# Mixture-of-experts tail of an attention kernel: the order in which POOL issues row gathers and row scatters

## The reference, cut to what is computed

```python
x = layernorm(x + attention(x))          # 2 batches x 1024 tokens x 128, 8 heads, differential attention
# the expert layer, E = 8 experts, cap = 256 tokens per expert and batch
probs = softmax(x @ gate_w)
top_p, top_idx = top_k(transpose(probs), cap)
xin = take_along_axis(x, top_idx)        # the rows that each expert chose
h = gelu(xin @ w1)                       # 128 -> 512
y = (h @ w2) * top_p                     # 512 -> 128
out = zeros().at[top_idx].add(y)         # rows added back where they came from
x = layernorm(x + out)
```

## Time and profile before

| what | us |
|---|---|
| median of 3 runs | 1060.2 |
| lowest, highest of them | 1058.76, 1063.17 |
| the profiled execution's own time | 1051.25 |
| its span, first to last instruction | 1049.5 |
| expert stage: first gather to the landing of the last scatter | 907.88 to 1028.70 |

### The profile page before, as it was taken

One profiled execution on the slowest core, in us unless ns is written; L12 is line 12 of the kernel. 1 busy time (PEld: TensorE's weight loads), 2 busy tenths in 40 slices (PEclk: granted clock), 3 DMA queues, 4 the chain that ended last, 5 costly groups with the idle time before them and its releaser, 6 DMA issues.

```text
span 1049.5 us, 15335 instructions
## 1 busy us (share of the span) xinstructions
PE 888.1 (85%) x4365; PEld 718.0 (68%) x4366; DVE 764.1 (73%) x1183; ACT 581.7 (55%) x1090; POOL 795.6 (76%) x874
## 2 busy tenths in 40 slices
PE   6789999999999999999999999999999732386700
PEld 5577778787877788778877887878788631165500
DVE  6777788877887878788778877888788547574303
ACT  3556667666766576656765666766676331143100
POOL 2567878887888798888888888888799753377762
PEclk9999999999999999999999999999999955599755
DMA  2000000000000000000000000000000152012223
GB/s 71 1 11 11 1 1 22 1 1 0 20 0 0 10 10 0 0 10 10 0 0 10 10 0 0 10 0 0 1 1 1 47 137 65 19 51 36 27 26 87
DMA packets 31856, 18.57 MB, mean 18 GB/s; under 512 B 4512, under 2 KB 30272, under 8 KB 31824
## 3 DMA queue, kind: packets, MB, share of 16 engines
q1 hardware_dynamic: 26192, 13.85, 4.8%
q0 software_dynamic: 5632, 4.33, 3.0%
HBM read 12.80 MB, written 5.37 MB: 17 GB/s over the span
## 4 chain that ended last, share of the span: by engine, by line
PE 53%; issue 17%; DVE 16%; POOL 7%; DMA 4%; ACT 3%; POOLq 0%; DVEq 0%; ACTq 0%; SPq 0%
PE t_ps L1061 7%; DVE negmax L750 6%; PE ring_a L994 5%; PE ring_b L994 5%; PE ring_a L996 5%; PE ring_a L995 5%; PE ring_b L996 4%; PE ring_b L995 4%; PE u_ps L994 4%; PE u_ps L996 4%; PE u_ps L995 4%; POOL acc_dram L491 3%; DMA acc_dram<-at,idx 2%; POOL prob L482 2%; ACT prob L562 2%
## 5 line engine op out<-in xcount | busy, mean ns | idle before, releaser
L449 POOL TENSOR_TENSOR at_lo<-at,at_hi 128x1024 fp32r<-128x1024 f32 x127 | 308.5, 2429 | 0.8
L562 ACT ACTIVATE prob<-ring_a,negmax 128x1024 f32<-128x1024 f32 x128 | 142.9, 1116 | 253.4 <-DVE negmax L750 253.4
L421 POOL TENSOR_TENSOR s1sq<-psum 128x1 f32<-128x1 f32 x127 | 104.4, 822 | 122.0 <-ACT at L570 120.4
L818 DVE SCALAR_TENSOR_TENSOR attn<-prob,coef 128x1024 f32<-128x1024 f32 x128 | 181.7, 1419 | 5.0
L750 DVE TENSOR_REDUCE negmax<-ring_b 128x1 f32<-128x1024 f32 x128 | 155.6, 1216 | 4.1 <-PE ring_b L996 1.2
L750 DVE TENSOR_REDUCE negmax<-ring_a 128x1 f32<-128x1024 f32 x128 | 155.6, 1216 | 1.1
L562 ACT ACTIVATE prob<-ring_b,negmax 128x1024 f32<-128x1024 f32 x128 | 143.0, 1117 | 19.5 <-DVE negmax L750 17.7
L424 POOL TENSOR_SCALAR at_hi<-at 128x1024 fp32r<-128x1024 f32 x127 | 142.4, 1122 | 0.0
L1061 PE MATMUL t_ps<-ident,attn 128*128 128x128 f32 x1024 | 133.7, 273 | 3.2 <-DVE attn L818 2.8
L1061 PEld LDWEIGHTS t_ps<-ident,attn 128*128 128x128 f32 x1024 | 118.3, 141 | 25.9 <-DVE attn L818 11.9
L570 ACT ACTIVATE at<-t_ps 128x1024 f32<-128x1024 f32 x128 | 130.3, 1018 | 2.0 <-PE t_ps L1061 2.0
(11 more groups left out here) (239 smaller groups left out, 1703.2 us busy)
## 6 DMA issues: line engine op xcount, KB each, us to landing
at<-in_L_ffn_w SPq DMA_DIRECT2D x16, 256.0 KB, 3.3
xres<-in_L_attn_X SPq DMA_DIRECT2D x2, 512.0 KB, 4.4
wq_s<-in_L_attn_Wq SPq DMA_DIRECT2D x8, 128.0 KB, 2.1
wk_s<-in_L_attn_Wk SPq DMA_DIRECT2D x8, 128.0 KB, 2.3
wv_s<-in_L_attn_Wv SPq DMA_DIRECT2D x8, 128.0 KB, 2.1
wo_s<-in_L_attn_Wo SPq DMA_DIRECT2D x8, 128.0 KB, 2.3
xg_dram<-xres SPq DMA_DIRECT2D x2, 512.0 KB, 3.4
acc_dram<-xres SPq DMA_DIRECT2D x2, 512.0 KB, 5.2
```

What stands on the lines that cost most here:

```text
L421: pool.tensor_tensor(s1sq[:, r % TPH:r % TPH + 1], s1, s1, ALU.mult).then_inc(s1sq_ready, 1)
L449: pool.tensor_tensor(at_lo[:, g, :, c], src, at_hi[:, g, :, c].bitcast(F32), ALU.subtract).then_inc(at_split, 1)
L562: act.activation(prob[:, par, m, :], ring[m][:, :], ACT.Exp, bias=negmax[:, par, m:m + 1], accum_out=sums).then_inc(prob_ready, 1)
L818: dve.scalar_tensor_tensor(out=attn[:, par, :], in0=prob[:, par, 1, :], scalar=coef[:, par:par + 1], in1=prob[:, par, 0, :], op0=ALU.mult, ...
```

## The change

POOL gathers only the experts 0 to 3 first (`AHEAD` = 4), and then issues scatter 0, gather 4, scatter 1, gather 5, scatter 2, gather 6, scatter 3, gather 7, and scatters 4 to 7. No transfer is added or taken away: 32 gathers and 32 scatters as before. The slots, the waits inside `gather` and `scatter`, and the order of the other engines stay.

```diff
     XSLOTS = 7
+    AHEAD = 4
...
-            for e in range(XSLOTS):
+            for e in range(AHEAD):
                 gather(e)
-            scatter(0)
-            for e in range(XSLOTS, E):
-                gather(e)
-            for e in range(1, E):
+            for e in range(E):
                 scatter(e)
+                if e + AHEAD < E:
+                    gather(e + AHEAD)
```

## The result

The median went from 1059.72 us (four runs) to 1078.57 us (four runs): slower by 18.85 us, ratio 1.017, 95% interval 1.0144 to 1.0195. The forecast was 1082.6, between 1076 and 1090.

What follows compares the result with a forecast made beforehand. The prediction took a chain of scatters, each waiting for the previous landing, as the bound. Four turns of 18.37 us (73.5) start scatter 4 22.4 us later; 1060.2 + 22.4 = 1082.6 us, range 1076 to 1090.

Steps and rivals of the forecast that it cites:

- the loop: Scatter e, gather e + 4, rows_in, scaling of e + 1, scatter e + 1: four turns of 18.37 us; 87%.
- landing pace: From scatter 4 on, each scatter waits for the previous one's landing: 9.64 us a link, 37.94 to the last landing.
- Release to first issue: From the scaling's end on DVE to POOL's first scatter issue: 0.85 us a turn, bounds 0.82 and 1.03.
- Four scatter issues: POOL's four issues of one scatter, partly beside DVE work: 7.70 us a turn, between 7.46 and 7.88.
- First to fourth gather: POOL, from a gather's first issue to its fourth: 4.10 us a turn, floor 3.93.
- Fourth gather to the transposes: From POOL's fourth gather issue to PE's transposes of the landed rows: 2.57 us a turn.
- Transposes to the scaling's end: From PE's transposes at half clock through DVE's subtraction and scaling: 3.15 us a turn, 2.65 at full clock.
- upper bound with the longest gather issues: Four turns with long landings, slow scatter issues and releases, plus every gather issue at its longest: loss of 33.7 us.
- The rival of held-up issues: Each of DVE's four casts a turn holds up a POOL issue: turns 2.1 us longer, loss 30.7, 1090.9 us; 7%.
- a gain of 7.15 us: Scatter 0 on POOL no longer waits behind the gathers of experts 4 to 6 and starts 7.15 us earlier.
- the step that carried the 8.95 us: The 8.95 us from the profiled execution's 1051.25 to the median 1060.2 was added unscaled to the forecast.
- The best that the forecast saw for this interleaving: Rival: scalings ready in time, POOL's own issues set turns of 13.1 us, 1061.6 us, no change; 4%.

Runs made afterwards that it cites:

- either order alone: Changed kernel with only PE handling the old expert ahead of the new: 1079.7 us, ratio 1.0168; with only DVE doing so: 1076.47 us, ratio 1.0165.
- turning both: Changed kernel with PE's rows_out and DVE's scaling of the old expert put ahead of the new expert's rows: 1062.75 us against 1061.21 before, ratio 1.0007.
- the pair on POOL: Changed kernel with POOL, after the same wait for expert e's scaling, issuing gather e + 4 ahead of scatter e: 1060.87 us against 1060.29 before, ratio 1.0019.
- five ahead: Changed kernel with AHEAD = 5 in place of 4, nothing else: 1058.34 us against 1060.29 before, ratio 0.9992.
- spread: Changed kernel with AHEAD = 5, PE and DVE taking old experts first, remaining gathers issued three behind each of scatters 0 to 3: 1059.86 us, ratio 1.0019.
- six ahead: Changed kernel with AHEAD = 6 in place of 4, nothing else: 1060.04 us against 1061.21 before, ratio 0.9984.

## Why the prediction was right

**The mechanism, step by step.** That the wait for a scaling now stands ahead of gathers, and that PE's and DVE's orders make that scaling wait for the gather behind it, is shown: either order alone keeps the loop, turning both, or the pair on POOL, opens it, with the same gathers and scatters otherwise. That the scatters behind scatter 4 go at landing pace is shown by the links of 10.1, 9.6 and 9.7 us; the forecast had 9.64 for the first.

**The terms of a turn.** Release to first issue: forecast 0.85; expert 0's scaling ended at 941.93 and scatter 0 started at 942.76, 0.83. Four scatter issues: forecast 7.70; 951.08 - 942.76 = 8.32, then 7.83, 7.84 and 8.14, a mean of 8.03. First to fourth gather: 4.10; 4.06 three times and 4.28. Fourth gather to the transposes: 2.57; 957.74 - 955.14 = 2.60, then 2.59 to 2.65. Transposes to the scaling's end: 3.15; 960.81 - 957.74 = 3.07, at half clock (four transposes in 1.13). The four turns made 74.55 against 73.5. (The forecast's upper bound with the longest gather issues, 33.7, adds up to 33.6.) The one term that was a little short is the scatters' issue beside DVE: line 492 in the changed kernel, as lowest, median and highest,

```profile
L492 POOL DMA_INDIRECT acc_dram<-at,idx x32: 1552/1592/2121, 942.8 to 1052.2; - x32
```

with the longest, 2.12 us, in the first turn. Four issues with DVE idle take 7.44 (scatter 5), so DVE's work costs 0.6 us a turn, of which the forecast's 7.70 held 0.26. The rival of held-up issues exists at that size and not at 2.1, and its mechanism was not quite the one named: it had each of the four casts (L957) of a turn hold up an issue. What counts in the rows is the operation that DVE has in progress when an issue starts, and mostly that is the subtraction on the gelu (L959). The longest scatter after, and a gather before that no cast overlaps:

```profile
944.64 0.69 DVE L959 TENSOR_TENSOR q_lo<-attn,q_hi 128x512 fp32r<-128x512 f32 x1
```

```profile
944.70 2.12 POOL L492 DMA_INDIRECT acc_dram<-at,idx  x1 [0.31 <-issue]
```

```profile
943.65 0.69 DVE L959 TENSOR_TENSOR q_lo<-attn,q_hi 128x512 fp32r<-128x512 f32 x1
944.26 0.68 DVE L947 TENSOR_TENSOR xk_lo<-u_ps,xk_hi 128x512 fp32r<-128x512 f32 x1
```

```profile
943.69 1.53 POOL L482 DMA_INDIRECT prob<-xg_dram,idx  x1 [0.30 <-issue]
```

Apart from the first gather in each, 45 issues of the 13 profiles are more than 0.25 us longer than the shortest of their kind. In 42 of them a subtraction of L959 was in progress at the start, in 3 a cast, and the extra time is 0.03 to 0.13 us less than what was left of it. Beside some 30 more issues the subtraction had begun only a few hundredths of a us earlier; there the subtraction was the longer one, 0.74 us or more against 0.69, and not the issue. Where L947 or the scaling, which read PSUM, was in progress, no issue was more than 0.07 us longer. That is read from the rows; no run took the subtractions away. The Trainium skill (SBUF — State Buffer, section "A bandwidth-pool intuition that's wrong (but worth ruling out)") has its example grow fivefold beside a copy, and puts that down to a block until the DVE operation ends and not to a slower transfer. The rows agree with a block by their size: no scatter issue of the changed kernel took more than 37% longer than the shortest, 0.57 us beside an operation of 0.69.

**Scatter 0** was forecast 31.8 us behind the first gather and came at 33.4. PE ran at the half clock level, 1.2 GHz, through nearly all of up(0) and most of up(1) in this execution, with products 0.43 us apart; in the first profile of before it was at the full one in up(1), with products 0.23 us apart. That is 1.6 us which the change didn't bring.

**The price.** The stage was forecast at 31.8 + 73.5 + 37.9 = 143.2 and took 146.0. The forecast of +22.4 is too high against the median's 18.85 for the other end of the difference: "The gathers of experts 4 to 6 push scatter 0 back by about 8 us" held for the one profile at hand, where scatter 0 started at 39.0. In three further profiles it started at 43.9, 47.6 and 47.5. Against their stages of 126.8, 130.4 and 129.4, the stage after, of which there is one profile, is longer by 19.2, 15.6 and 16.7 us, against the first by 25.2; the mean of the four is 19.2, near the 18.85 of the medians. The term "a gain of 7.15 us" is thus mis-sized: against the three further profiles, starting scatter 0 early is worth 10.5 to 14.2 us. The loop costs the 30 us or so by which its four turns exceed those of before, and part of that is paid back.

The same holds for the step that carried the 8.95 us between the profiled execution and the median over to the new median unchanged. Most of such a difference lies in the stage: of the four profiled executions of before, the stage takes 6.0 to 9.6 us more in the three further ones, while what lies outside the stage differs by 3.1 at most (930.4 to 933.5). The changed kernel, with 16 gathers in a row, does not have these late scalings. So two misses point opposite ways, a stage after that is 2.8 us longer than forecast and a stage before that is usually 6 to 9.6 us longer than the one profiled, and that the number came within 4.0 us is in part luck. The loop and the length of its turns are not.

**Where it would have been wrong.** The best that the forecast saw for this interleaving, 1061.6 us with POOL's own issues as the pace, is what came of opening the loop: 1062.75 with both orders turned and 1060.87 with the gather first. Their stages, 130.4 and 126.7, are longer than the 122.2 that it stands for, as those of before are.

## What to carry to other kernels

A wait in an engine's order holds all that stands behind it: before moving a prefetch behind a dependent store on one queue, follow that store's data back through every engine's order, and see whether it runs through the prefetch of a later turn; if it does, the look-ahead is shorter than its number says. Four experts ahead were in effect none, because the two engines behind POOL take the new rows ahead of the old results; with five ahead, or with the gather ahead of the scatter in the same pair, no scatter waited for it. And when a difference of a few per cent is forecast from one profile of before, a second and a third profile of the same kernel show which of its terms hold.

## What was not expected of the hardware

While many indirect gathers run in a row, ACT's waits for PE end late. The longest delay from PE's end to ACT's start among the gelu parts, the roundings and the copies of the first experts was 0.9, 0.9, 1.0, 2.3 and 2.5 us in five profiles with 16 gathers in a row, and 2.2 where the rest was held back behind 16; 4.2 and 3.9 us with 20 (five ahead, and spread); 9.2 with 24 (six ahead); 12.1, 14.9 and 14.7 in three profiles of before with 28, and 0.1 in its first. These delays are sums over several waits; no single wait marked "remote" is longer than 5.85 us. Holding the gathers back after 16 brought expert 0's scaling from 43 to 47 down to 33.8 us, in one run. So the delay goes with the run of gathers in 12 of 13 profiles. What delays the release is not shown: the trace has no record of the releaser, one profile with 28 gathers is free of it, and scatters in a row show nothing of the kind. Whether it is in the transfers' own semaphores or in the recording of so many of them stays open, and was not tried.
